# Feed-forward of a decoder kernel: tiles taken in pairs, inner values turned as fp32, tokens quantised by halves

## The reference

```
    def _L0_ffn_ref(x, w_gate, w_up, w_down):
        ...
        def _act_quant(x):
            scale = 127.0 / jnp.clip(jnp.max(jnp.abs(x), axis=-1, keepdims=True), 1e-05)
            xq = jnp.clip(jnp.round(x * scale), -128.0, 127.0) / scale
            return x + jax.lax.stop_gradient(xq - x)
        def _bitlinear(x, w):
            return jnp.einsum('bsi,oi->bso', _act_quant(x), _weight_quant(w))
        gate = jax.nn.silu(_bitlinear(x, w_gate))
        up = _bitlinear(x, w_up)
        return _bitlinear(gate * up, w_down)
```

## Time and profile before

| | |
|---|---|
| median of 3 runs | 1829.61 us (1823.79 to 1832.76) |
| the profiled execution | 1830.69 us, of which the traced span is 1829.0 us |
| feed-forward's norm | 392.15 to 402.50 us |
| its front, up to the first `hid` | 402.5 to 417.76 us |
| its tiles, from the first `hid` to the last add | 417.76 to 468.94 us |
| next stage's norm (`n4`) | 469.26 to 481.89 us |

### The profile page before, as it was taken

The page is one execution under the profiler, slowest core; times in us unless marked ns, Lnnn a source line. Parts: engine busy times, 40 slices in busy tenths (PEclk is TensorE's granted clock), DMA queues, the critical chain, the costliest instruction groups (busy, mean ns, idle before and its releaser), DMA issues. The chain is left out here.

```text
span 1829.0 us, 23410 instructions
## 1 busy us (share of the span) xinstructions
PE 1330.1 (73%) x6866; PEld 650.4 (36%) x6867; DVE 1443.8 (79%) x2463; ACT 1106.2 (60%) x2434; POOL 1141.3 (62%) x742
## 2 busy tenths in 40 slices
PE   6777998966757557767557657557645798899878
PEld 4554555643222112222112222112201555565523
DVE  4664888877259999999999999999996577777634
ACT  4444887856565566665566665566643677677630
POOL 2111665640079999999999999999993244444400
PEclk9998999995678777787777878778867799999979
DMA  3000000000054443353454343444224111211000
GB/s 98 1 2 1 2 2 1 1 25 1 6 221 152 184 185 145 122 192 128 184 191 160 133 161 132 186 185 173 106 103 137 48 47 50 91 46 47 1 0 23
DMA packets 70218, 168.04 MB, mean 92 GB/s; under 512 B 20420, under 2 KB 40152, under 8 KB 56664
## 3 DMA queue, kind: packets, MB, share of 16 engines
q1 hardware_dynamic: 68680, 166.17, 24.5%
q10 hardware_dynamic: 1168, 0.53, 0.1%
q0 software_dynamic: 256, 0.01, 0.0%
HBM read 131.03 MB, written 35.65 MB: 91 GB/s over the span
## 5 line engine op out<-in xcount | busy, mean ns | idle before, releaser
L1586 POOL TENSOR_TENSOR ma_hs<-ma_dtuR,ma_Bt 128x1024 f32<-128x1024 f32 x256 | 597.0, 2360 | 30.4 <-PE ps L1663 23.3
L1769 ACT ACTIVATE ps<-ma_dtR,ma_A 128x512 f32<-128x512 f32 x512 | 332.6, 682 | 314.3 <-DVE ma_hs L1911 271.5
L844 POOL TENSOR_TENSOR x_pr<-x_pr,x_rec 128x512 f32<-128x512 f32 x256 | 267.7, 1046 | 293.1 <-DVE x_rec L1084 293.1
L1905 DVE TENSOR_TENSOR_SCAN ps<-ps,ma_hs 128x1024 f32<-128x1024 f32 x176 | 401.8, 2283 | 1.9 <-POOL ma_hs L1586 1.8
L1050 ACT ACTIVATE x_pr<-x_sm,x_mx 128x256 f32<-128x256 f32 x512 | 255.3, 500 | 71.6 <-DVE x_mx L1075 68.9
L1663 PE MATMUL ps<-ma_hs,ma_fold 128*32 128x512 f32 x1024 | 163.9, 770 | 163.2 <-POOL ma_hs L1594 151.0
L1911 DVE TENSOR_TENSOR ma_hs<-ps,ma_Ct 128x1024 f32<-128x1024 f32 x176 | 215.4, 1224 | 6.1
L1905 DVE TENSOR_TENSOR_SCAN ma_hs<-ps,ma_hs 128x1024 f32<-128x1024 f32 x80 | 182.5, 2281 | 31.0 <-ACT ps L1769 28.7
L1630 PE MATMUL ps<-ma_hn,ma_w_tap 128*128 128x512 f32 (+3 forms) x256 | 145.1, 721 | 79.0 <-ACT ma_hn L1793 79.0
L1594 POOL TENSOR_TENSOR ma_hs<-ma_hs,ma_Ct 128x1024 f32<-128x1024 f32 x80 | 188.5, 2356 | 13.5 <-DVE ma_hs L1905 13.5
L906 PE MATMUL ps<-ident,x_pr 128*128 128x128 f32 x1024 | 163.2, 286 | 5.8 <-DVE x_pT L984 4.6
(11 more groups left out here) (307 smaller groups left out, 2222.6 us busy)
## 6 DMA issues: line engine op xcount, KB each, us to landing
ma_dtuR<-ma_dtu_d SPq DMA_DIRECT2D x32, 1024.0 KB, 6.8
ma_dtR<-ma_dt_d SPq DMA_DIRECT2D x32, 1024.0 KB, 8.9
ma_Bt<-ma_bc_d SPq DMA_DIRECT2D x16, 1024.0 KB, 4.9
ma_Ct<-ma_bc_d SPq DMA_DIRECT2D x16, 1024.0 KB, 7.4
ma_dtu_d<-ma_dtu SPq DMA_DIRECT2D x32, 256.0 KB, 2.0
ma_dt_d<-ma_dt SPq DMA_DIRECT2D x32, 256.0 KB, 2.3
keys_d<-ma_kv SPq DMA_DIRECT2D x32, 256.0 KB, 5.0
values_d<-ma_kv SPq DMA_DIRECT2D x32, 256.0 KB, 2.6
```

The source lines that it names most:

```text
L844: pool.tensor_tensor(pr[:, r, :, :], pr[:, r, :, :], rec[:, r, :].unsqueeze(2).broadcast_to([P, 2, L]), ALU.mult).then_inc(pr_done, 1)
L1586: pool.tensor_tensor(hs[:, k % SLOTS, :, :], dtuR[:, unit(f, h), q, :].unsqueeze(1).broadcast_to([P, 2, CH]), rows(Bt, k), ALU.mult).then_ ...
L1769: e = act.activation(c.ps[:, 2 * (k % 2) + a, :], dtR[:, unit(f, h), q, :], ACT.Exp, scale=A[:, (f // QUARTERS) % 2, h, q, no:no + 1])
L1905: dve.tensor_tensor_scan(out, pair(k), slot(k), 0.0, ALU.mult, ALU.add).then_inc(scan_done, 1)
```

## The change

Five things change, all in `ffn_stage`.

1. **No separate `hq`.** PE turns `hr` itself, as fp32 with the fp32 identity, into bank 4 (even tiles) or bank 7 (odd tiles). ACT's copy out of PSUM takes ROUND off and writes bf16 `hqT`. ACT's L1262 goes; ACT's copy becomes an fp32 read with a bias.
2. **Pairs.** Each engine's list goes by pairs j of tiles: the small instructions of a pair are one each (128x2), the output's two turns are added to `xT` in one 128x256 add, and the skew is counted in pairs (the down product and output of pair j-1 stand in step j, and DVE adds pair j-2).
3. **No hardware loop.** All eight pairs are written out; addresses are constants.
4. **Halves.** The tokens are quantised in two halves of two chunks (`quantise`), and gate and up of tile 0 stand ahead of the turns of the second half.
5. **The table** that Silu needs is loaded ahead of the token copies (`preload_act_table_set`).

```
@@ def ffn_stage(c, g): @@
-        ht = s.sb("ht", [P, 2, 4])
+        ht = s.sb("ht", [P, 2, 4, 2])
-        hq = s.sb("hq", [P, 2, F], BF16)
...
+        def turn_bank(t):
+            return 4 + 3 * (t % 2)
...
+                def gate_up(t):
+                    pe.wait_ge(xqT_done, t // TB + 1)
+                    if t < 2:
+                        pe.wait_ge(xr_done, 2 * t + 2)
+                    else:
+                        pe.wait_ge(hid_done, t - 1)
+                    for i in range(2):
+                        pe.matmul(c.ps[:, 2 * (t % 2) + i, :], xqT[:, t * P:(t + 1) * P], c.wguT[:, i * F:(i + 1) * F],
                                   start=True, stop=True).then_inc(gu, 1)
-                        pe.wait_ge(hq_done, t)
...
-                            mm = pe.transpose(c.psb(4)[:, k * P:(k + 1) * P], hq[:, 1 - p, k * P:(k + 1) * P], c.identb[:, :])
+                def turn_hidden(t):
+                    pe.wait_ge(hr_done, t + 1)
...
+                    for k in range(4):
+                        mm = pe.transpose(c.ps[:, turn_bank(t), k * P:(k + 1) * P], hr[:, t % 2, k * P:(k + 1) * P], c.ident[:, :])
+                    mm.then_inc(hr_turned, 1)
...
+                turn_tokens(0)
+                turn_tokens(1)
+                gate_up(0)
+                turn_tokens(2)
+                turn_tokens(3)
+                gate_up(1)
+                for j in range(NPAIR + 1):
+                    if j + 1 < NPAIR:
+                        gate_up(2 * j + 2)
+                        gate_up(2 * j + 3)
+                    if j >= 1:
+                        down_projection(j - 1)
+                    if j < NPAIR:
+                        turn_hidden(2 * j)
+                        turn_hidden(2 * j + 1)
+                    if j >= 1:
+                        turn_output(j - 1)
...
-                        act.activation(hq[:, 1 - p, :], hr[:, 1 - p, :], ACT.Identity, bias=less[:, 0:1]).then_inc(hq_done, 1)
...
-                        act.activation(hqT[:, 1 - p, :, :].rearrange("p k q -> p (k q)"), c.psb(4)[:, 0:F],
-                                       ACT.Copy).then_inc(hqT_done, 1)
+                def hidden(t):
+                    act.wait_ge(hr_turned, t + 1)
+                    if t >= 2:
+                        act.wait_ge(down, t // 2)
+                    act.activation(hqT[:, t % 2, :, :].rearrange("p k q -> p (k q)"), c.ps[:, turn_bank(t), :],
+                                   ACT.Identity, bias=less[:, 0:1]).then_inc(hqT_done, 1)
...
+                act.preload_act_table_set("silu_and_others")
+                tokens(0)
+                tokens(1)
+                act.wait_ge(unit_done, 4)
+                gates(0)
+                tokens(2)
+                tokens(3)
+                gates(1)
...
+                for j in range(NPAIR + 1):
+                    if j + 1 < NPAIR:
+                        gates(2 * j + 2)
+                        gates(2 * j + 3)
+                    if j >= 1:
+                        outputs(j - 1)
+                    if j < NPAIR:
+                        hidden(2 * j)
+                        hidden(2 * j + 1)
...
+                def quantise(half):
+                    chunks = range(2 * half, 2 * half + 2)
...
+                    dve.wait_ge(top_done, 2 * half + 2)
+                    dve.tensor_scalar(unit[:, tt], top[:, tt], 1e-5, 1.0 / 127.0, ALU.max, ALU.mult).then_inc(unit_done, 1)
...
+                quantise(0)
+                quantise(1)
+                for j in range(NPAIR):
+                    b = j % 2
+                    for t in (2 * j, 2 * j + 1):
                         dve.wait_ge(gate_done, t + 1)
                         dve.wait_ge(gu, t * 2 + 2)
...
+                        dve.scalar_tensor_tensor(out=hid[:, t % 2, :], in0=c.ps[:, 2 * (t % 2) + 1, :], scalar=s_up[:, t:t + 1],
+                                                 in1=gate[:, t % 2, :], op0=ALU.mult, op1=ALU.mult).then_inc(hid_done, 1)
+                    for t in (2 * j, 2 * j + 1):
                         dve.wait_ge(hid_done, t + 1)
+                        dve.tensor_reduce(ht[:, b, 0, t % 2:t % 2 + 1], hid[:, t % 2, :], AX.X, ALU.max,
+                                          apply_absolute_value=True).then_inc(ht_top, 1)
+                    dve.wait_ge(ht_top, 2 * j + 2)
+                    dve.tensor_scalar(ht[:, b, 1, :], ht[:, b, 0, :], 1e-5, 1.0 / 127.0, ALU.max, ALU.mult).then_inc(ht_unit, 1)
+                    if j >= 2:
+                        add_output(j - 2)
...
+                add_output(NPAIR - 2)
+                add_output(NPAIR - 1)
```

More of the change, by code:

```diff
@@ L1207, in _, with turn_tokens @@
                     mm.then_inc(turned, 1)
-                for a in range(NB):
+                def turn_tokens(a):
                     pe.wait_ge(xq_done, a + 1)
@@ L1222, in step @@
                                   start=True, stop=True).then_inc(gu, 1)
[L1223 removed]
+                def turn_hidden(t):
+                    pe.wait_ge(hr_done, t + 1)
+                    pe.wait_ge(xqT_done, NB)
+                    if t >= 2:
                         pe.wait_ge(hqT_done, t - 1)
[L1225 to L1229 removed]
@@ L1246, in _, with tokens @@
                 norm.on_scalar(act)
-                for a in range(NB):
+                def tokens(a):
                     act.wait_ge(xq_turned, a + 1)
                     act.activation(xqT[:, a * CH:(a + 1) * CH], c.psb(4 + a)[:, 0:CH], ACT.Copy).then_inc(xqT_done, 1)
-                act.wait_ge(less_set, 1)
[L1252 to L1261, removed]
-                        act.activation(hq[:, 1 - p, :], hr[:, 1 - p, :], ACT.Identity, bias=less[:, 0:1]).then_inc(hq_done, 1)
[L1263 to L1266, removed]
-                        act.activation(hqT[:, 1 - p, :, :].rearrange("p k q -> p (k q)"), c.psb(4)[:, 0:F],
-                                       ACT.Copy).then_inc(hqT_done, 1)
[L1269 to L1273, removed]
@@ new lines, in outputs @@
+                def outputs(j):
+                    act.wait_ge(down, j + 1)
+                    act.wait_ge(ht_out, j + 1)
+                    if j >= 1:
+                        act.wait_ge(y_turned, j)
+                    for t in range(2):
+                        act.activation(y[:, t, :], c.ps[:, DOWN, t * P:(t + 1) * P], ACT.Copy,
+                                       scale=ht[:, j % 2, 3, t:t + 1]).then_inc(y_done, 1)
+                act.preload_act_table_set("silu_and_others")
+                tokens(0)
@@ L1279, in _ @@
                 dve.memset(less[:, :], -ROUND).then_inc(less_set, 1)
[L1280 to L1295, removed]
@@ L1328 @@
+                    dve.wait_ge(ht_inv, j + 1)
+                    for t in (2 * j, 2 * j + 1):
+                        if j >= 1:
+                            dve.wait_ge(hr_turned, t - 1)
+                        dve.tensor_scalar(hr[:, t % 2, :], hid[:, t % 2, :], ht[:, b, 2, t % 2:t % 2 + 1], ROUND,
+                                          ALU.mult, ALU.add).then_inc(hr_done, 1)
+                add_output(NPAIR - 2)
+                add_output(NPAIR - 1)
 class RecurrentWeights:
```

113 lines of the change are left out of this document (55 added, 58 removed).

## The result

| | before | after |
|---|---|---|
| median | 1831.11 us (1823.79 to 1832.76, 4 runs) | 1806.64 us (1803.5 to 1811.85, 4 runs) |
| the profiled execution's span | 1829.0 us | 1804.8 us |
| feed-forward with its norm | 392.15 to 469.26: 77.1 us | 393.17 to 451.32: 58.15 us |
| next norm, `n4` | 12.95 us | 12.36 us |
| last layer's expert stage | 73.95 us | 68.28 us |

The ratio is 0.9872, 95% interval [0.9856, 0.9888]. A stage is counted from PE's first product in it to PE's first product in the next (so `n4` before runs to 482.21, where the table further up ends it at 481.89). Of 24.2 us between the two spans, 19.0 lie in the feed-forward, 0.6 in `n4` and 5.7 in the expert stage, whose code did not change; the rest differs by 1.0 the other way, for the most part because the feed-forward was reached 1.02 us later. The medians lie 24.5 us apart.

What follows compares the result with a forecast made beforehand. ACT's and DVE's lists were taken as nearly closed at 3.0 us a tile, DVE binding after. Gains 13.85 (pairs and tail), 3.65 (front) and 0.5 (`n4`) sum to 18.0 us: median 1811.6 us, range 1806 to 1819.

Steps and rivals of the forecast that it cites:

- the clock up into `n4`: Norm behind the stage: PE's clock still high there, up to 2.3 us to gain; part of the 1806 end.
- DVE, 4.07 us a pair: Feed-forward pairs: DVE's instruction strides add up to 4.07 us a pair, against 6.0 for two tiles before.
- ACT's copy, 0.68: Pairs: ACT's copy, now reading fp32 in PSUM with a bias, takes 0.68 us, between 0.60 and 0.72.
- The front: Token quantisation up to the second `hid`: it starts at 416.4 instead of 420.05, gain 3.65 us.
- The three cases: Front, by POOL's hold: `unit` held, second `hid` 417.4; nothing held, 414.2; only first `xq` held, 415.5.
- the remark that it would cost 1.28 without the cover: Front: the table load falls where ACT is idle and costs nothing; without that cover, 1.28 us.
- The clock: Pairs: PE's clock rises from 0.50 to 1.00 within the first three pairs, near 424 to 427, and stays up.
- The first rival: Pairs: clock stays low and PE bounds at 4.6 us a pair, 1815 to 1817 us; chance 0.2.
- the cover by the skew: First three pairs: gates made one pair ahead hide PE's low-clock 4.65 us against DVE's 4.07.
- Behind the stage, 0.5: `n4`'s first eight products: up to 2.3 us to gain if the clock is still up; 0.5 taken.
- The reading of the bound: Tiles of the kernel before: ACT's and DVE's lists both nearly closed at 3.0 us, loop instructions included.
- the closed ring: PE's list: gates behind turns add 3.3 us a pair, P = 7.4, 1834 us; chance 0.03 with dear turns.

Runs made afterwards that it cites:

- e3: Changed kernel with `hq` put back (ACT rounds into bf16, PE turns bf16) against the kernel before: 4.05 us a pair, ratio 0.9904.
- e12: Changed kernel with the table load back at its old place ahead of the first gate: second `hid` 24.35 us, stage 59.50 us, one run.
- e11: Kernel before with the sixteen fp32 turns of `xn` made four times over, 64 in a row: the row took 8.88 us, one run.
- e6: Changed kernel run and profiled once more, nothing altered, against the kernel before: ratio 0.9864, second `hid` 24.34 us, stage 59.48 us.
- e1: Kernel before with only its hardware loop written out, against the kernel before: 5.90 us a pair, ratio 0.9979.

## Why the prediction was right

Forecast 1811.6 us (1806 to 1819), measured 1806.64. The forecast gain of 18.0 stands against 19.6 and 20.1 in stage and `n4` of the traces: the mechanism and its size were right. It stands against 24.5 between the medians, and that 1806.64 fell inside the range, 0.6 us from its end, is luck in part: that end was set by two things, nothing held at the front and the clock up into `n4`, and the 4 to 5 us that brought the median there came from elsewhere.

- **DVE, 4.07 us a pair**: 4.03 measured, no idle time of DVE. Right, and made of the strides between the written-out tiles. From the second `hid` to the last add's end 35.05 was forecast; 450.99 - 416.16 = 34.83 came.
- **ACT's copy, 0.68**: 0.683.
- **The front**: second `hid` at 416.4, 24.25 from the stage's start. It came at 22.99 and at 24.34. The three cases were right in kind, since `xq` or a small instruction is held until POOL ends, but the instruction in the race is `s_up`, not `unit`: `unit` takes 0.17 us in both profiles, ahead of POOL's long instruction. (In e3, begun 0.16 us behind a short copy of POOL's, it took 0.28 and ended 0.03 behind the copy.)
- **The table load**: its place costs nothing, but the remark that it would cost 1.28 without the cover was wrong; with the tokens in halves DVE is on the second half then (e12). With the tokens in one piece no run has it at the old place.
- **The clock**: rightly high, but the route was right at most in part. I had the backlog of fp32 turns raise it near 424 to 427. In the first profile it rose at 417.6, behind token turns and first products, before any `hr` had been turned. In the second it rose at 421.1, behind the first eight turns of `hr` and the products after them:

```profile
414.70:421.10 6.40, 4.89 (x16) 2.48 (x16) 6.26 (x16) 3.55 (x6) 0.00 (x0) 0.50 0.01 3
421.10:449.50 28.40, 18.86 (x155) 13.09 (x155) 25.46 (x64) 19.47 (x41) 0.00 (x0) 1.00 0.00 1
```

  In e3, with bf16 turns, it rose only at 425.3. That fp32 turns alone can raise it is shown by e11, against the rule in the Trainium skill, "TensorE: Matmul & The Clock Gate", section "Part 4: PE-mode transpose", that a transpose does not count; no run has bf16 turns alone. The first rival did not come about, and its price, 4.6 us a pair, stays untested, since no run held the clock low through the pairs. The one pair nearly all at the low level, the second of e6, took 3.82 us, as the changed kernel's at the high level; that fits the cover by the skew. The turns cost 0.11 at the high level and not 0.13.
- **Behind the stage, 0.5**: 0.6 and 2.3 in the two profiles, by whether the clock had fallen in the tail.
- **What the sum lacked**: the other 4 to 5 us between the medians. In the first pair of profiles the expert stage alone differed by 5.7, by a pattern of the clock that comes and goes. A term for the scatter of later stages belonged into the range.
- **The reading of the bound**: I had both lists closed at 3.0 us a tile and the loop's instructions in them. e1 shows 0.04 us a tile from these. In the waits of the kernel before from 425.5 to 461.6, DVE stood idle 2.2 us in 11 times ahead of `hid`, and 3.2 us in 11 times ahead of L1320 for ACT's `y`, so its list was less full than I read it.
- **A slip**: the five terms of the closed ring add up to 3.2 us and not 3.3; nothing rests on it.

## What to carry to other kernels

Where an engine's list alternates with another engine's answer, listing two tiles' worth of each step lets the second tile cover the first one's round trip; here that took a pair from 5.9 to 4.05 us (e1 and e3), and dropping an instruction from the same list added little after it. Count the new period from starts of neighbouring instructions in written-out code, engine by engine, and take the largest. When a program's parts run at a clock that goes up and down, compare stages of the traces, not only totals, and profile each kernel twice.

## What the runs showed of the hardware

- An instruction of DVE on 8 elements a row took 2.86 us instead of 0.23, because it was issued 0.01 us after a long one of POOL's (e6). Whether it came ahead went with PE's clock in six profiles: a fall a few tenths of a microsecond earlier made the turns that DVE waits for later.
- In the expert stage PE was busy 16.5 of 17.0 us and the granted clock stayed at 0.50 (1.2 GHz) all that time, before the change and in e6 after it, and then rose under the same products; sixty-four fp32 turns had it up after 3.8 us.
